# A four-layer graph network on one core: degrees turned by PE, an earlier square root, a factor row from three bf16 parts

## What is computed

```python
row, col = edge_index + one more loop per node
deg = segment_sum(1, col)
dis = where(deg > 0, rsqrt(max(deg, 1)), 0)
conv(x, W, b)[i] = sum over edges (j -> i) of dis[j] * dis[i] * (x @ W)[j] + b
x = layernorm(x + conv(relu(conv(x, W1, b1)), W2, b2))
```

## Time and profile before

| | us |
|---|---|
| median of 3 runs | 894.0 (893.34 to 897.51) |
| profiled execution, its own time | 898.61 |
| its span, first to last instruction | 896.8 |
| PE busy | 819.1 (91%) |
| DVE busy | 606.7 (68%) |
| ACT busy | 324.9 (36%) |
| mean granted clock of PE | 0.963 of 2.4 GHz |

### The profile page before, as it was taken

One profiled execution on the slowest core, in us unless ns is written; L12 is line 12 of the kernel. 1 busy time (PEld: TensorE's weight loads), 2 busy tenths in 40 slices (PEclk: granted clock), 3 DMA queues, 4 the chain that ended last, 5 costly groups with the idle time before them and its releaser, 6 DMA issues.

```text
span 896.8 us, 16138 instructions
## 1 busy us (share of the span) xinstructions
PE 819.1 (91%) x6422; PEld 726.5 (81%) x6422; DVE 606.7 (68%) x927; ACT 324.9 (36%) x578; POOL 12.5 (1%) x35
## 2 busy tenths in 40 slices
PE   7399999999976999999989997989997999999995
PEld 5299999999976999799989996444545999689994
DVE  3598999999946766678877862557556554235554
ACT  0134544444455222342344221244324322432242
POOL 2200000000000000000000000000000000000000
PEclk9997999999997999999998998999998999999998
DMA  9845888887840000000000000000000000000001
GB/s 273 171 95 123 171 182 176 184 182 170 179 94 20 1 1 1 1 1 1 1 11 10 1 1 3 1 0 12 1 1 23 1 0 1 0 1 1 1 24 50
DMA packets 167388, 48.57 MB, mean 54 GB/s; under 512 B 155034, under 2 KB 165854, under 8 KB 167307
## 3 DMA queue, kind: packets, MB, share of 16 engines
q1 hardware_dynamic: 154176, 45.36, 21.8%
q10 hardware_dynamic: 12012, 0.83, 0.9%
q0 software_dynamic: 1120, 1.29, 0.6%
HBM read 45.44 MB, written 8.41 MB: 60 GB/s over the span
## 4 chain that ended last, share of the span: by engine, by line
PE 83%; DVE 7%; DMA 3%; issue 3%; ACT 2%; SPq 2%; DVEq 0%; ACTq 0%
PE bank L1650 19%; PE bank L1651 19%; PE bank L1586 14%; PE bank L1576 10%; PE bank L1848 2%; DMA lists_d<-in_src 2%; PE bank L1785 2%; PE bank L1856 2%; PE bank L1837 2%; PE bank L1710 1%; PE bank L1836 1%; DVE tmp L1233 1%; PE bank L1900 1%; PE bank L1899 1%; PE bank L1789 1%
## 5 line engine op out<-in xcount | busy, mean ns | idle before, releaser
L1650 PE MATMUL bank<-stage,f_hi 125*128 125x392 f32 x1000 | 350.1, 350 | 8.4 <-DVE wb L1125 4.8
L1651 PE MATMUL bank<-stage,f_lo 125*128 125x392 f32 x1000 | 343.6, 344 | 0.0
L1092 DVE CAST stage<-counts 125x2352 fp32r<-125x2352 uint8 x120 | 164.7, 1380 | 85.9 <-PE bank L1651 85.7
L1650 PEld LDWEIGHTS bank<-stage,f_hi 125*128 125x128 f32 x1000 | 190.8, 191 | 10.7 <-issue 9.9
L776 ACT ACTIVATE stage<-counts 125x1568 fp32r<-125x1568 uint8 x80 | 108.1, 1351 | 237.8 <-PE bank L1651 235.5
L1651 PEld LDWEIGHTS bank<-stage,f_lo 125*128 125x128 f32 x1000 | 190.7, 191 | 0.6
L1586 PE MATMUL bank<-tmp,wb 128*65 128x25 f32 x2000 | 135.3, 223 | 0.2 <-DVE tmp L1044 0.2
L1586 PEld LDWEIGHTS bank<-tmp,wb 128*65 128x65 f32 x2000 | 132.0, 147 | 0.7 <-DVE tmp L1044 0.5
L730 ACT ACTIVATE counts<-bank 125x500 uint8<-125x500 f32 x188 | 87.8, 536 | 44.7 <-PE bank L1576 43.8
L1576 PE MATMUL bank<-rowb,xT 128*128 128x125 bf16 x1250 | 90.1, 229 | 7.3 <-DVE rowb L1024 3.8
L1021 DVE TENSOR_TENSOR xT<-xT,tmp 128x2560 bf16<-128x2560 bf16 (+1 forms) x63 | 92.7, 1472 | 3.2 <-PE bank L1576 1.9
(11 more groups left out here) (211 smaller groups left out, 696.7 us busy)
## 6 DMA issues: line engine op xcount, KB each, us to landing
wb<-in_edge_attr SPq DMA_DIRECT2D x125, 256.0 KB, 3.8
lists_d<-in_dst SPq DMA_DIRECT2D x1, 3104.0 KB
lists_d<-in_src SPq DMA_DIRECT2D x1, 3104.0 KB
wa<-in_x SPq DMA_DIRECT2D x12, 125.0 KB
out<-wl SPq DMA_DIRECT2D x6, 250.0 KB
xT<-in_dst SPq DMA_DIRECT2D x63, 4.0 KB, 3.5
xT<-in_dst ACTq DMA_DIRECT2D x62, 4.0 KB, 3.3
wb<-in_L_gnn_w_ih SPq DMA_DIRECT2D x1, 384.0 KB, 3.5
```

What stands on the lines that cost most here:

```text
L1092: nc.vector.tensor_copy(set_buffer(u, m), counts[:, SETS[u][0]:sum(SETS[u]), chunk(pair * 2 + off)]).then_inc(s["set_d_ready"], 1)
L1650: mm(bank[h][:, 0:CH], f_hi[:, first + k, :], rhs[:, k, :], start=(first + k == 0), stop=False)
L1651: last = mm(bank[h][:, 0:CH], f_lo[:, first + k, :], rhs[:, k, :], start=False, stop=(first + k == HI - 1))
```

## The change

Four edits in the stretch between counting and first sum:

- The store of the degrees and their three loads go. PE turns the degrees itself, by 25 transposes of one row of 125 into one column each, in bank 3, ahead of the node transposes; DVE copies the 25 columns to `dis_col`. The flag's matmul moves from behind the raw weights to ahead of the sixth group of node transposes. PE's general branch moves ahead of the fold, and so does the wait of POOL's.
- ACT takes a square root of a constant behind the node copies, so the table is loaded there; the square root of the degrees comes behind the raw weights, and the upper halves follow. The folded weights and biases are kept only behind the upper halves.
- DVE splits the factors in three bf16 parts (four operations, `dis_split`) behind the scaling. Masks and bias split move behind the lower halves.
- PE spreads the row from the three bf16 parts, three matmuls for each tile that add into the same place, in place of one in fp32.

```diff
+DEG_AT = 64
...
+        dis_rest = tmp[:LO, 3, 32:32 + HI]
+        dis_part = tmp[:LO, 3, 64:64 + 3 * HI].bitcast(BF16)[:, 0:3 * HI].rearrange("p (k h) -> p k h", k=3)
...
-            sp.wait_ge(s["ea_kept"], NGP)
-            sp.dma_start(deg_d.rearrange("(a n) -> a n", a=1), eaT[DE:DE + 1, :]).then_inc(s["deg_out"], 16)
             sp.wait_ge(s["unit_kept"], NU)
             sp.wait_ge(s["ea_made"], NE)
...
-            sp.wait_ge(s["deg_out"], 16)
-            degrees_to_tiles(s["deg_in"])
-            sp.wait_ge(s["fold_kept"], 2)
-            sp.dma_start(gate_w_d, gate_w).then_inc(s["ws_out"], 16)
             taken = flag_of(sp)
             with sp.If(taken):
...
+            sp.wait_ge(s["fold_kept"], 2)
+            sp.dma_start(gate_w_d, gate_w).then_inc(s["ws_out"], 16)
...
-            general_sources(pool, 0, taken, [("fold_kept", 2), ("xt_kept", NGR)])
+            general_sources(pool, 0, taken, [("raw_kept", 3), ("xt_kept", NGR)])
...
+            nc.scalar.activation(small[:, 0:1], mean_w[:, :], ACT.Sqrt)
             for g in range(3):
                 n = 4 if g < 2 else 1
                 act.wait_ge(s["raw_t"], g + 1)
...
+            act.wait_ge(s["in_ready"], 1)
+            nc.scalar.activation(dis_tmp[:, :], in_inv[:, :], ACT.Sqrt).then_inc(s["sqrt_made"], 1)
+
+            xn = wa[:LO, :].rearrange("p (h f) -> p h f", h=HI)
+            for i, (g, n) in enumerate(GROUPS):
+                act.wait_ge(s["nodes_made"], i + 1)
+                nc.scalar.activation(f_hi[:, g:g + n, :], xn[:, g:g + n, :], ACT.Copy).then_inc(s["f_hi_made"], 1)
...
             act.wait_ge(s["fold_made"], 3)
             nc.scalar.activation(bias_f, bank[2][bias_rows, 0:3 * D], ACT.Copy).then_inc(s["bias_kept"], 1)
...
-            act.wait_ge(s["in_ready"], 1)
-            nc.scalar.activation(dis_tmp[:, :], in_inv[:, :], ACT.Sqrt).then_inc(s["sqrt_made"], 1)
...
             keep_row(0)
...
-            dve.wait_ge(s["deg_in"], 48)
+            dve.wait_ge(s["deg_t"], 1)
+            nc.vector.tensor_copy(dis_col[:, :], bank[3][:LO, DEG_AT:DEG_AT + HI]).then_inc(s["deg_t"], 1)
+            dve.wait_ge(s["deg_t"], 2)
...
+            nc.vector.tensor_copy(dis_part[:, 0, :], dis_col[:, :]).then_inc(s["dis_split"], 1)
+            dve.wait_ge(s["dis_split"], 1)
+            nc.vector.tensor_tensor(dis_rest, dis_col[:, :], dis_part[:, 0, :], ALU.subtract).then_inc(s["dis_split"], 1)
+            dve.wait_ge(s["dis_split"], 2)
+            nc.vector.tensor_copy(dis_part[:, 1, :], dis_rest).then_inc(s["dis_split"], 1)
+            dve.wait_ge(s["dis_split"], 3)
+            nc.vector.tensor_tensor(dis_part[:, 2, :], dis_rest, dis_part[:, 1, :], ALU.subtract).then_inc(s["dis_split"], 1)
+
+            dve.wait_ge(s["unit_kept"], NU)
+            dve.wait_ge(s["pad_made"], 2)
+            first_sets(0)
+            for i, (g, n) in enumerate(GROUPS):
+                dve.wait_ge(s["f_hi_made"], i + 1)
+                nc.vector.tensor_tensor(f_lo[:, g:g + n, :], xn[:, g:g + n, :], f_hi[:, g:g + n, :].bitcast(F32),
+                                        ALU.subtract).then_inc(s["f_lo_made"], 1)
+            dve.wait_ge(s["const_made"], 7)
+            for m, a in ((C_MIN, BIAS_AT), (C_MOUT, BIAS_AT + PARTS)):
...
             dve.wait_ge(s["bias_kept"], 1)
             dve.wait_ge(s["masks_made"], 1)
...
+            pe.wait_ge(s["ea_kept"], NGP)
+            for h in range(HI):
+                last = nc.tensor.transpose(bank[3][:LO, DEG_AT + h:DEG_AT + h + 1], eaT[DE:DE + 1, tile_nodes(h)], ident[DE:DE + 1, DE:DE + 1])
+            last.then_inc(s["deg_t"], 1)
             pe.wait_ge(s["x_in"], 16 * (PAIRS + 1))
...
+                if i == 5:
+                    pe.wait_ge(s["flag_part"], 2)
+                    mm(bank[3][0:1, 0:1], g_any[:LO, :], mean_w[:LO, 0:1], start=True, stop=True).then_inc(s["flag_made"], 1)
...
+            taken = flag_of(pe)
+            general_products(pe, 0, taken, [("xt_kept", NGR), ("raw_kept", 3)])
             pe.wait_ge(s["raw_kept"], 3)
...
-            def spread(bnk, col, n):
+            def spread(bnk, parts, n):
 
                 for h in range(n):
-                    last = mm(bnk[:, h * LO:(h + 1) * LO], col[:, h:h + 1].to_broadcast([LO, D]), ident[:LO, :LO], start=True, stop=True)
+                    for k in range(3):
+                        last = mm(bnk[:, h * LO:(h + 1) * LO], parts[:, k, h:h + 1].to_broadcast([LO, D]), ident_bf[:LO, :LO], start=(k == 0), stop=(k == 2))
                 return last
...
-            pe.wait_ge(s["dis_ready"], 1)
-            row(0, dis_col)
+            pe.wait_ge(s["dis_split"], 4)
+            row(0, dis_part)
```

More of the change, by code:

```diff
@@ L217, in gnn_program @@
             "edges_in x_in w_in const_made far_made tail_out table_out last_made starts_made idx_made pool_w dve_w act_w "
[L218 to L219 removed]
+            "slots_clean list_made list_t list_kept lo_hot key_hot dst_hot unit_made unit_kept ea_made ea_kept deg_t "
+            "dis_split raw_in raw_t raw_kept xt_made xt_kept f_hi_made f_lo_made nodes_made set_d_ready set_d_used set_a_ready "
             "set_a_used sum_kept fm_done fm_kept fm_more pre_made gate_h norm_t norm_var norm_sd norm_scale norm_za norm_zd "
@@ L749, in _ @@
                 nc.scalar.activation(wl1[:, (3 + 4 * g) * D:(3 + 4 * g + n) * D], bank[g][:, 0:n * D], ACT.Copy).then_inc(s["raw_kept"], 1)
[L750 to L753, removed]
             act.wait_ge(s["in_ready"], 1)
@@ L767, in keep_row @@
                     nc.scalar.activation(at_nodes(rowb[:, g * LO:(g + n) * LO], n), by_node(bank[4 + k % 4][:, 0:n * LO], n), ACT.Copy).then_inc(s["row_kept"], 1)
+            act.wait_ge(s["fold_made"], 3)
+            nc.scalar.activation(bias_f, bank[2][bias_rows, 0:3 * D], ACT.Copy).then_inc(s["bias_kept"], 1)
+            for k, (g, n) in enumerate(((0, 4), (4, 2))):
+                nc.scalar.activation(wl1[:, (3 + g) * D:(3 + g + n) * D], bank[k][:, 0:n * D], ACT.Copy).then_inc(s["fold_kept"], 1)
             keep_row(0)
@@ L1059, in _ @@
             nc.vector.tensor_tensor(g_any[:LO, :], g_most[:LO, :], g_bad[:LO, :], ALU.max).then_inc(s["flag_part"], 1)
[L1061 to L1065, removed]
             dve.wait_ge(s["flag_made"], 1)
@@ L1097, in first_sets @@
                 conv(q, 0, 0, 2)
+            nc.vector.tensor_copy(dis_part[:, 0, :], dis_col[:, :]).then_inc(s["dis_split"], 1)
[14 more added lines that the diff above has]
+            for m, a in ((C_MIN, BIAS_AT), (C_MOUT, BIAS_AT + PARTS)):
+                nc.vector.tensor_reduce(cols[:, m:m + 1], ident[:, a:a + PARTS], AX.X, ALU.add)
+            nc.vector.tensor_reduce(cols[:, C_MID:C_MID + 1], ident[:, BIAS_AT:BIAS_AT + 2 * PARTS].rearrange("p (k n) -> p k n", k=2)[:, :, 1:3], AX.XY, ALU.add)
+            nc.vector.tensor_reduce(cols[:, C_LOW:C_LOW + 1], ident[:, BIAS_AT + 2:BIAS_AT + 2 * PARTS:PARTS], AX.X, ALU.add).then_inc(s["masks_made"], 1)
             dve.wait_ge(s["bias_kept"], 1)
@@ L1106, in _ @@
                 dve.wait_ge(s["bias_split"], 2 if m is mid else 4)
[L1108 to L1114, removed]
             def neighbour_sum(q, dest, more=None, then=None, unrolled=False, first_last=True, squared=False, early=None):
@@ L1608, in _ @@
                 last.then_inc(s["raw_t"], 1)
-            pe.wait_ge(s["flag_part"], 2)
-            mm(bank[3][0:1, 0:1], g_any[:LO, :], mean_w[:LO, 0:1], start=True, stop=True).then_inc(s["flag_made"], 1)
+            taken = flag_of(pe)
+            general_products(pe, 0, taken, [("xt_kept", NGR), ("raw_kept", 3)])
             pe.wait_ge(s["raw_kept"], 3)
@@ L1622, in _ @@
             last.then_inc(s["fold_made"], 1)
-            taken = flag_of(pe)
-            general_products(pe, 0, taken, [("xt_kept", NGR), ("fold_kept", 2), ("bias_kept", 1)])
             def sum_chunk(q, t, h, between=None, looking=False):
@@ L1687, in node_tiles, with row @@
                     last.then_inc(s["nodes_made"], 1)
-            def spread(bnk, col, n):
+            def spread(bnk, parts, n):
                 for h in range(n):
-                    last = mm(bnk[:, h * LO:(h + 1) * LO], col[:, h:h + 1].to_broadcast([LO, D]), ident[:LO, :LO], start=True, stop=True)
+                    for k in range(3):
+                        last = mm(bnk[:, h * LO:(h + 1) * LO], parts[:, k, h:h + 1].to_broadcast([LO, D]), ident_bf[:LO, :LO], start=(k == 0), stop=(k == 2))
                 return last
-            def row(i, col):
+            def row(i, parts):
                 for k, (g, n) in enumerate(GROUPS):
@@ L1699, in row @@
                         pe.wait_ge(s["row_kept"], NGR * i + k - 3)
-                    spread(bank[4 + k % 4], col[:, g:g + n], n).then_inc(s["row_made"], 1)
+                    spread(bank[4 + k % 4], parts[:, :, g:g + n], n).then_inc(s["row_made"], 1)
             def node_group(i, k, name, value):
```

## The result

The changed kernel takes 890.8 us (median of 22 runs, 887.42 to 896.47); the kernel before, run beside it, takes 898.75 (22 runs, 892.45 to 904.0). The ratio is 0.9926, with a 95% interval of 0.9909 to 0.9943: faster by 0.74%, or 6.7 us, with 5.1 to 8.2 as the interval. The forecast was 885.0, from a gain of 9.0. So the direction was right and the gain about a quarter smaller, and the time lies 0.1 above the top of the range (890.7).

What follows compares the result with a forecast made beforehand. Between counting and first sum, 28.3 us were bound by the degrees' DRAM way, the late square root and DVE's order; the sum starting at 280.0 instead of 289.0 gains 9.0 off the median 894.0: 885.0, range 882.0 to 890.7.

Steps and rivals of the forecast that it cites:

- Degrees by PE, at full clock: Between counting and fold: 25 transposes of degrees on PE replace the DRAM way, 2.8 us, nodes' transposes behind them 2.86.
- rival B: PE's transposes or row run at the lower clock: gain 4.0 or 5.0, a part of either 6.5; chance 0.17.
- Square root early: ACT loads table and takes root ahead of the kept fold; DVE multiplies at 270.45 instead of 278.78, 8.33 us earlier.
- The covers: Ahead of ACT's root, raw weights, flag with reciprocal, and PE's branch stay hidden behind other work, with 1.3 to 2.5 us spare.
- DVE's order and lag: DVE splits in 0.8, allows the sum at 279.4; later masks and bias split leave 0.4 of its 2.60 wait for PE.
- rival A: DVE's lag from masks and bias split comes through in the first sum: gain only 6.8, 887.2 us; chance 0.13.
- Row: PE's spreading ahead of the first sum: 75 bf16 instructions right behind the fold at full clock, 4.4 us, sum starts at 280.0.
- rival C: In the row, load and matmul don't overlap: 24.9 us, start 11.4 later, 905.4 us, slower; chance 0.05.
- Rival D: Something else, weights or a branch whose code comes late, holds the sum and hides the gain, over 4.5 us; chance 0.02.

Runs made afterwards that it cites:

- after: The first profile of the changed kernel, no further edit; from first transpose behind counting to first matmul of the first sum it takes 23.4 us, against 28.3 before.

## Why the prediction came out as it did

**Degrees by PE, at full clock: the step that failed.** The prediction took 2.8 for 25 and put the nodes' 2.86 behind it unchanged. At full clock the form costs 3.03 to 3.06, so its price was near enough. What was mis-sized is the clock over both groups: in four profiles of the change the degrees took 5.17 once and 3.03 to 3.16 otherwise, the nodes 4.6 to 5.6 each time. The evidence against rival B was that before, the clock stood at 1.00 through 267.5, 6 us after counting; but that showed the clock behind *nodes'* transposes, and the change put other work in their place. The six profiles with nodes first kept it for 4.9 to 7.0 us, the eight with degrees first for 0.3 to 3.3, with no overlap. The Trainium skill, "TensorE: Matmul & The Clock Gate", Part 4 (PE-mode transpose), says that transposes don't count as busy for the clock in the way matmuls do. For the degrees the trace leans that way; for the nodes' transposes less so, since they ran at 1.00 to their end (2.86) in all five profiles in which all 25 stood first. The rule does not tell the two apart, and here the difference decided.

**The sum with the true terms.** In the three later profiles the factors came at 11.3 instead of 9.75 (1.55: the nodes cost some 1.9 more, the degrees 0.2 more, and ACT's part behind them 0.5 less) and the way from there to the sum took 10.75 instead of 9.55 (1.2): 19.3 + 1.55 + 1.2 = 22.05, as measured. In the first profile the factors lost 4.55 and the rest gained 0.45: 23.4. The gain in the stretch is thus 4.9 to 6.3, next to the measured 6.7 (5.1 to 8.2), whose interval covers the difference. That is rival B, which had a chance of 0.17 as a whole, at the price that it put on a part of either stage (6.5). Against the three runs' 894.0 the time would have stood at 887.5, inside the range. But the kernel before was at 898.75 over 22 runs, of which those three are the first; its profiled execution (898.61) had hinted at it. So a second term was wrong, the base from which the gain was taken off: its 4.75, and not the mechanism, moved the time from inside the range to just above it.

**Square root early: right.** Table, raw weights and root follow the node copies in the order forecast and in 1.28, 1.23 and 0.24, close to what was forecast, only as late as the nodes made them. Undoing it cost 4 to 5.5 us of the stretch. The covers held: in after, ACT never waited for raw weights or reciprocal.

**DVE's order and lag: right.** Split 0.85 (0.8 forecast). DVE's wait for PE was 0.44 (0.4 forecast) where the row ran at full clock; in the three profiles in which the row met the lower clock it was 2.05, since PE came later. DVE waits for PE in both cases, so rival A is out.

**Row: half right.** 75 instructions in 4.29 at full clock (4.4 forecast), so rival C is out. But "the row follows the fold without such a wait" failed: PE waited 0.74 to 2.24 for the split in every profile of the change, since the fold, 3.0 at full clock, is shorter than the scaling and split beside it; and in three of four the lower clock came into the row (5.91).

**Rival D** is out: no wait for weights or code stands in after's chain over the stretch.

## What to carry to other kernels

Where PE has only transposes to do, ask what comes directly behind the last dense matmuls: the order of the same transposes moved the granted clock's fall by 3 to 6 us here, and everything that queued behind them moved with it. Put on the critical path's head what kept the clock in the trace, and let the clock fall where another engine is the bound anyway. A clock read from a row of before holds for that work and not for what the change puts in its place.

And before a gain is taken off a median, look at how the profiled execution stands to it: here the median of three runs lay 4.75 below that of twenty-two.

## What the runs showed of the hardware

- A transpose of one row into one column costs as much as one of 125 rows: 3.03 to 3.06 for 25 degrees, 2.86 for 25 node tiles, at 1.00. The Trainium skill, "TensorE: Matmul & The Clock Gate", Part 2 (LDWEIGHTS), says that a weight load's time goes with its columns and not with its rows; these two durations agree with it, since the degrees load 1 row of 125 columns and the nodes 125 rows of 128.
- Alternating the one-row fp32 transposes with 128-row bf16 matmuls was dear: 0.36 for a pair at full clock, where the transpose alone starts every 0.12 and the matmul, in counting, every 0.059. What makes the pair so slow was not tried.
- The clock's fall is not the same in each execution of one program: 0.3, 2.8, 3.3 and 2.9 us after the first transpose in four profiles of the change. What about the one-row transposes brings it on is open.
